# Routed expert blocks of a decoder layer: turning the token rows by VectorE instead of TensorE, and the order of the work beside it

## The reference, cut to what matters

```
x = x + mamba_branch(layernorm(x))                       # 8 x 512 tokens, 256 features
x = x + cross_attention(layernorm(x), ctx, ctx)
xf = layernorm(x)                                        # 4096 x 256
shared = gelu(xf @ Wfc_s + bfc_s) @ Wproj_s + bproj_s
topk_p, topk_i = top_k(softmax(xf @ Wr), 2)              # 2 of 8 experts, normalized
for e in range(8):
    h = gelu(xf @ Wfc[e] + bfc[e]) @ Wproj[e] + bproj[e] # 256 -> 1024 -> 256
    routed += h * gate[:, e]
x = x + shared + routed
```

## Time and profile before

| | |
|---|---|
| median of 3 runs | 934.13 us (933.46 to 935.68) |
| profiled execution | 939.65 us, span 938.0 us |
| TensorE busy, share of span | 901.5 us, 96% |
| VectorE busy | 611.6 us, 65% |
| ScalarE busy | 518.8 us, 55% |
| GpSimd busy | 338.4 us, 36% |
| mean granted clock | 0.99 |
| DMA | 64.0 MB in 48943 packets, mean 68 GB/s |

### The profile page before, as it was taken

How to read it: one execution, slowest core, us unless ns; L and a number is a source line. 1 busy time by engine, 2 the same in 40 slices (tenths; PEclk the granted TensorE clock), 3 DMA queues, 4 the chain that set the end, 5 groups by cost and what they waited for, 6 DMA issues and landing times.

```text
span 938.0 us, 20267 instructions
## 1 busy us (share of the span) xinstructions
PE 901.5 (96%) x6934; PEld 794.0 (85%) x6943; DVE 611.6 (65%) x1457; ACT 518.8 (55%) x1050; POOL 338.4 (36%) x318
## 2 busy tenths in 40 slices
PE   6999998999998999999999899999999999999996
PEld 4688995566655788888889899999999999999996
DVE  4898796898877766666555655565565656565442
ACT  3693433665546355546444666575666657575552
POOL 3467222211311554544453224233242423332222
PEclk9999999999999999999999899999999999999998
DMA  8300020000002111111237245225252522522222
GB/s 240 123 1 1 1 91 1 2 1 1 2 16 84 49 71 59 65 60 59 77 114 249 58 135 135 47 45 136 46 136 46 136 46 46 136 46 46 46 46 35
DMA packets 48943, 64.00 MB, mean 68 GB/s; under 512 B 9984, under 2 KB 41920, under 8 KB 48768
## 3 DMA queue, kind: packets, MB, share of 16 engines
q0 software_dynamic: 17504, 34.87, 16.0%
q1 hardware_dynamic: 31248, 27.46, 9.9%
q10 hardware_dynamic: 144, 1.05, 0.4%
HBM read 38.59 MB, written 24.77 MB: 68 GB/s over the span
## 4 chain that ended last, share of the span: by engine, by line
PE 86%; DVE 7%; issue 3%; ACT 1%; DMA 1%; POOL 1%; SPq 1%; DVEq 0%; POOLq 0%; ACTq 0%
PE PS L136 24%; PE PS L137 23%; PE PS L138 23%; PE PS L877 3%; PE PS L1833 2%; PE PS L306 2%; PE PS L907 1%; PE PS L921 1%; PE PS L927 1%; DVE mxpad L1121 1%; DVE hidl L142 1%; PE PS L287 1%; DMA xr<-routed_rows 1%; PE PS L1360 1%; PE PS L849 1%
## 5 line engine op out<-in xcount | busy, mean ns | idle before, releaser
L1879 ACT ACTIVATE hideh<-PS,be 128x256 fp32r<-128x256 f32 x280 | 140.5, 502 | 154.2 <-PE PS L138 139.5
L1907 POOL DMA_INDIRECT out_rows<-y,toki x70 | 122.9, 1755 | 270.4 <-DVE y L1947 261.3
L142 DVE TENSOR_TENSOR hidel<-act32e,hideh 128x256 fp32r<-128x256 f32 x280 | 118.4, 425 | 107.5 <-ACT act32e L1881 95.3
L136 PE MATMUL PS<-xTeh,wfch 128*128 128x256 f32 x560 | 159.4, 285 | 1.7 <-issue 1.1
L136 PE MATMUL PS<-wprh,hideh 128*128 128x256 f32 x560 | 159.0, 284 | 0.0
L137 PE MATMUL PS<-xTel,wfch 128*128 128x256 f32 x560 | 158.4, 283 | 0.0
L138 PE MATMUL PS<-xTeh,wfcl 128*128 128x256 f32 x560 | 158.4, 283 | 0.0
L138 PE MATMUL PS<-wprh,hidel 128*128 128x256 f32 x560 | 155.9, 278 | 0.0
L137 PE MATMUL PS<-wprl,hideh 128*128 128x256 f32 x560 | 155.9, 278 | 0.0
L1881 ACT ACTIVATE act32e<-PS,be 128x256 f32<-128x256 f32 x280 | 140.9, 503 | 2.8 <-DVE hidel L142 2.8
L136 PEld LDWEIGHTS PS<-xTeh,wfch 128*128 128x128 f32 x560 | 107.3, 192 | 3.3 <-issue 2.6
(11 more groups left out here) (273 smaller groups left out, 2086.3 us busy)
## 6 DMA issues: line engine op xcount, KB each, us to landing
xr<-routed_rows SPq DMA_DIRECT2D x36, 272.0 KB
fcraw<-in_Wfc POOLq DMA_DIRECT2D x8, 1024.0 KB
prraw<-in_Wproj POOLq DMA_DIRECT2D x8, 1024.0 KB
X<-in_x SPq DMA_DIRECT2D x8, 512.0 KB, 6.6
out_rows<-X SPq DMA_DIRECT2D x8, 512.0 KB, 2.9
routed_rows<-pads SPq DMA_DIRECT2D x8, 272.0 KB
out_rows<-y,toki POOLq DMA_INDIRECT x70
ctx<-in_ctxT SPq DMA_DIRECT2D x4, 256.0 KB, 6.5
```

Of the source, the lines that this page charges most:

```text
L136: nc.tensor.matmul(out, wh, xh, start=first, stop=False)
L142: return eng.tensor_tensor(out, whole, high.bitcast(F32), ALU.subtract)
L1879: nc.scalar.activation(hid[0][:, j, :], PS[:, j % 4, 0:BLK], ACT.Gelu_apprx_tanh, bias=bias)
L1907: nc.gpsimd.indirect_dma_start(out=out, out_offset=bass.IndirectOffsetOnAxis(ap=toki[:, h:h + 1], axis=0), in_=y[:, h, :], in_offset=None, ...
```

## The change

The rows of a block are loaded as four DMAs instead of one. DMA q takes features 64q to 64q+63 of all 256 rows and puts them on the partitions 32q to 32q+31, each partition holding eight pieces of 256 bytes. One VectorE transpose then turns every 32x32 square of the 128x512 tile in place on its partitions: partition 32q+f holds features of quarter q, for all 256 tokens. So the features come in another order than before, and the rows of `Wfc` are reordered to match on the host. x_high and take now read `xt` in SBUF. The gates and token numbers come by a small DMA of their own (64 bytes a row), which ACT issues at the head of each block. The gate copy and the two bias products move from behind the h_lows into the gaps between them; `toki` is copied after take, and only that copy waits for `y_sent`. The split is cut finer: ACT does one piece before x_high and three behind it, VectorE's `wprl` becomes two pieces, and its pieces stand between turn, take and the outputs.

```diff
+            xb = first_rows("xb", [P, BLK // SQ, KD * SQ])
+            metar = first_rows("metar", [P, 2, ROW - D])
+            rgx = RG.rearrange("(n t j) c -> n j t c", t=BLK // SQ, j=SQ)
...
-                sp.dma_start(xr[:], rg[0].rearrange("p h c -> p h c")).then_inc(x_in, 16)
+                for q in range(P // SQ):
+                    sp.dma_start(xb[q * SQ:(q + 1) * SQ],
+                                 rgx[0, :, :, q * KD * SQ:(q + 1) * KD * SQ]).then_inc(x_in, 16)
...
-                    if b == B - 1:
-                        routed_first()
...
                     def load(g, e, par, i):
                         sp.wait_ge(xr_free, g + 1)
-                        sp.dma_start(xr[:].rearrange("p (a h) c -> p a h c", a=1),
-                                     rg[bass.ds(e * NBR + i, 1)]...).then_inc(x_in, 16)
+                        for q in range(P // SQ):
+                            sp.dma_start(xb[q * SQ:(q + 1) * SQ]..., rgx[row, :, :, ...]...).then_inc(x_in, 16)
...
-                def transposes(pe, g):
-                    pe.wait_ge(x_in, g * 16 + 16)
-                    for k in range(KD):
-                        for h in range(2):
-                            last = nc.tensor.transpose(PS[:, 4, ...], xr[:, h, k * P:(k + 1) * P], ident[:])
+                def turn(dve, g):
+                    dve.wait_ge(x_in, g * X_IN + X_IN)
+                    nc.vector.transpose(xt[:]..., xb[:]...).then_inc(xr_free, 1)
...
                     def x_high(g):
-                        act.wait_ge(x_psum, g + 1)
-                        nc.scalar.activation(xTp[0][:]..., PS[:, 4, :], ACT.Copy).then_inc(xT_high, 1)
+                        act.wait_ge(xr_free, g + 2)
+                        nc.scalar.activation(squares(0), xt[:]..., ACT.Copy).then_inc(xT_high, 1)
...
                     def gelus(g, e, par, i):
+                        act.wait_ge(gate_ready, g + 1)
+                        nc.scalar.dma_start(metar[:]..., rg[bass.ds(e * NBR + i, 1), :, :, D:ROW]...).then_inc(meta_in, 16)
...
+                        with act.If(i * E + e < E - 1):
+                            act.wait_ge(raw_in, e * 32 + 64)
+                            split_up(1 - par, 0)
                         x_high(g + 1)
                         with act.If(i * E + e < E - 1):
-                            act.wait_ge(raw_in, e * 32 + 64)
-                            split_high(1 - par)
+                            split_up(1 - par, 1)
+                            split_down(1 - par)
...
+                        h_low(range(5))
+                        dve.wait_ge(meta_in, g * 16 + 16)
+                        nc.vector.tensor_copy(gate[:], metar[:, :, bass.ds(e, 1)]...).then_inc(gate_read, 1)
+                        h_low(range(5, 6))
+                        scale_bias(0)
+                        h_low(range(6, 7))
+                        scale_bias(1).then_inc(bias_gated, 1)
+                        h_low(range(7, KH))
+                        turn(dve, g + 1)
                         with dve.If(i * E + e < E - 1):
+                            up_low(0)
+                        take(dve, g + 1)
+                        dve.wait_ge(y_sent, g + 1)
+                        nc.vector.tensor_copy(toki[:], metar[:, :, E]).then_inc(gate_ready, 1)
...
```

More of the change, by code:

```diff
@@ L47, in build @@
     BLK = 2 * P
+    SQ = 32
     SQ = 32
@@ L1503, in whole @@
                         act.wait_ge(raw_in, 32)
-                        split_high(0)
+                        for k in range(KD):
+                            split_up(0, k)
+                        split_down(0)
                     if b < B - 1:
@@ L1823, in routed_sync, with squares, first_turn @@
                     load(before + count, E - 1, 1, 0)
-                    sp.wait_ge(x_in, (before + count) * 16 + 16)
+                    sp.wait_ge(x_in, (before + count) * X_IN + X_IN)
                     sp.sem_inc(sp_waits, 1)
-                def transposes(pe, g):
-                    pe.wait_ge(x_in, g * 16 + 16)
-                    if not isinstance(g, int):
-                        pe.wait_ge(xT_ready, g)
-                    for k in range(KD):
-                        for h in range(2):
-                            last = nc.tensor.transpose(PS[:, 4, k * BLK + h * P:k * BLK + (h + 1) * P],
-                                                       xr[:, h, k * P:(k + 1) * P], ident[:])
-                    last.then_inc(x_psum, 1)
+                xt = Place(rows_at)("xt", [P, BLK // SQ, KD, SQ])
+                def squares(n):
+                    return xTp[n][:].rearrange("p k (t j) -> p k t j", j=SQ)
+                def first_turn(dve):
+                    dve.sem_inc(xr_free, 1)
+                    turn(dve, 0)
+                def turn(dve, g):
+                    dve.wait_ge(x_in, g * X_IN + X_IN)
+                    nc.vector.transpose(xt[:].rearrange("p t k j -> p (t k j)"),
+                                        xb[:].rearrange("p t c -> p (t c)")).then_inc(xr_free, 1)
                 def take(dve, g):
-                    dve.wait_ge(x_psum, g + 1)
                     dve.wait_ge(xT_high, g + 1)
-                    low(nc.vector, xTp[1][:].rearrange("p k n -> p (k n)"), PS[:, 4, :],
-                        xTp[0][:].rearrange("p k n -> p (k n)")).then_inc(xT_ready, 1)
-                    nc.vector.tensor_copy(meta[:], xr[:, :, D:ROW]).then_inc(xr_free, 1)
+                    low(nc.vector, squares(1), xt[:].rearrange("p t k j -> p k t j"),
+                        squares(0)).then_inc(xT_ready, 1)
                 def routed_tensor(pe):
@@ new lines, in down_low @@
+                        def down_low(k):
+                            dve.wait_ge(e_high, e * 2 * KD + 3 * KD + k + 1)
+                            ks = slice(k * KH // KD, (k + 1) * KH // KD)
+                            return low(nc.vector, wpr[1][:, 1 - par, ks], prraw[:, ks], wpr[0][:, 1 - par, ks])
+                        h_low(range(5))
+                        dve.wait_ge(meta_in, g * 16 + 16)
+                        nc.vector.tensor_copy(gate[:], metar[:, :, bass.ds(e, 1)].rearrange("p h a -> p (h a)")).then_inc(
+                            gate_read, 1)
@@ new lines, in one @@
+                        dve.wait_ge(y_sent, g + 1)
+                        nc.vector.tensor_copy(toki[:], metar[:, :, E]).then_inc(gate_ready, 1)
+                        with dve.If(i * E + e < E - 1):
+                            up_low(1).then_inc(e_low, 1)
+                        dve.wait_ge(bias_gated, g + 1)
+                        output(0)
+                        with dve.If(i * E + e < E - 1):
+                            down_low(0)
+                        output(1)
+                        with dve.If(i * E + e < E - 1):
+                            down_low(1).then_inc(e_low, 1)
@@ L1954, in routed_vector @@
                     dve.sem_inc(l_ready, 2)
                     every_block(dve, one)
-                return (routed_sync, routed_tensor, routed_scalar, routed_gpsimd, routed_vector), transposes, take
-            routed, first_transposes, first_take = routed_stage()
+                return (routed_sync, routed_tensor, routed_scalar, routed_gpsimd, routed_vector), first_turn, take
+            routed, first_turn, first_take = routed_stage()
             with nc.Block() as block:
```

78 lines of the change are left out of this document (39 added, 39 removed).

## The result

| | before | after |
|---|---|---|
| median of the runs | 933.8 us (932.8 to 935.68, 4 runs) | 925.83 us (925.64 to 926.33, 4 runs) |
| profiled execution, its span | 939.65, 938.0 us | 925.91, 924.3 us |
| regular block, up + transposes + down | 5.76 + 0.35 + 5.55 = 11.66 us | 5.70 + 0 + 5.65 = 11.35 us |
| block 1 starts at | 529.59 | 522.74 |

The ratio is 0.99 (0.9881 to 0.992), a saving of 8.0 us. Forecast were 916.5, a saving of 17.6, and the range of 912 to 924 doesn't hold the time. The sign was right, the size not.

A forecast was written before the change was run, and what follows sets the result against it. The prediction took TensorE to bound the routed stage, waiting for nobody. It summed 15.0 us for 34 blocks and 2.6 for block 0 to 17.6, giving 934.13 - 17.6 = 916.5 us, with an 8-in-10 range of 912 to 924.

The forecast's parts named there:

- 34 x 0.44 = 15.0: Routed blocks 1 to 34: taking the transposes off TensorE saves 0.44 us in each, 15.0 us in all.
- Free: Small DMA on ACT, head of each block: its 0.39 us issue fits ScalarE's idle time before the first gelu.
- The term for block 0, 2.6: Block 0 and what leads up to it: block 1 starts 5.1 us earlier, about 2.5 comes back, 2.6 kept.
- Transposes on the path: Routed stage: each block's transposes stand in TensorE's chain as a piece of 0.44 us.
- Rival 1: Between up and down: a new wait takes the transposes' place; 931.5 us if all 0.44 returns, 924 if half; chance 0.08.
- Gate copy and bias products at nothing: Among the h_lows: gate copy and two bias products fit VectorE's 0.31 us gaps; cost nothing if nothing overlaps.
- Rival 3: Blocks behind a split or load, about 14: late ACT chain or late gates, some 1 us each; 930.5 us; chance 0.07.
- Turn, x_high, take: Between up and the next up: VectorE's turn, x_high and take stay hidden, at least 1.1 us to spare.
- Split at nothing: Weight split, cut finer: costs nothing; if the cover fails, at most 2.4 us in 7 blocks.
- rival 2: Row loads can't keep the pace: slower from landing times of 9.1 us or so, about 967 at 10; chance 0.06.
- the rule on 512 bytes: Row loads in 256-byte pieces: by the skill's rule they land later, block 0 gains only 0.2, total 918.9 us.
- The saving is taken over to the median: Final sum: the 17.6 us saving, counted on a profile 5.5 us above the median, is subtracted from median 934.13.

The follow-up runs named there:

- e2: Changed kernel with 128 unused bytes behind xb, putting the routed stage's tiles back at their old addresses; 926.38 us, ratio 0.9906.
- e3: Changed kernel with the gate copy and both bias products moved from among the h_lows to behind take; 924.19 us, ratio 0.9884.
- e7: Changed kernel with the small DMA issued by SP one block ahead and token numbers copied aside; 921.26 us, ratio 0.9853.
- e4: Changed kernel with four transposes of a constant tile put back on TensorE between up and down; 937.27 us, ratio 1.0027.
- e17: Changed kernel with 64 bytes ahead of the small tile and nothing else; 922.64 us, ratio 0.9862.
- e6: Changed kernel with VectorE's turn and its loads, but gate work, toki and the whole split behind the h_lows; 932.43 us, ratio 0.9972.
- e11: Changed kernel with gate copy and bias products still in the gaps, but the split in one piece as before; 932.49 us, ratio 0.9971.
- e12: Changed kernel with the split still spread, but gate copy, toki and bias products behind take; 923.53 us, ratio 0.9886.
- e10: Kernel before with its four transposes done twice in blocks 1 to 34; 946.8 us (one run).
- e9: Kernel before with the transposes of blocks 1 to 34 reading a constant tile instead of the rows; 932.46 us (one run).
- e13: Changed kernel with four constant transposes between up and down and 128 bytes ahead of the small tile; 932.79 us (one run).
- e14: Changed kernel with the small DMA on SP a block ahead, plus 64 bytes ahead of the small tile; 913.62 us (one run).
- e15: Changed kernel with the small DMA on SP a block ahead and 64 bytes ahead of the small tile, timed again in rounds; 916.11 us, ratio 0.9795.
- e5: Kernel before with the four transposes left out of every routed block, nothing else changed; 928.31 us, ratio 0.9912.
- e16: Changed kernel with the small DMA on SP a block ahead, xTe shifted by 64 bytes and hide by 128; 913.59 us, ratio 0.9778.
- e1: Kernel before, unchanged, run once more for a second profile; 934.65 us, span 933.0.

## Why the prediction failed

Two steps failed, of nearly equal size. Either alone would have left the time inside 912 to 924 (about 922); together they put it outside.

The first failed step is the term "34 x 0.44 = 15.0". It priced what leaves and took the spacing of what stays from the old stream ("Without transposes the distance is two steps", and "48 x 0.1135" for down without them). Measured: down's spacing goes from 0.1137 to 0.1177 when the transposes go (0.25 saved, not 0.44, by the removal alone), and up's from 0.120 to 0.1187 since the removed `metae` tile moves everything behind it by 128 bytes (e2 takes that back). That is 0.315 a block, 34 x 0.315 = 10.7, 4.3 less than the term.

The second failed step is the price of nothing for the gate work in the gaps ("if nothing overlaps: nothing") and for the small DMA ("Free"). It left out the wait for that DMA. Measured: five downs behind weight loads lose 3.85 us in the changed kernel's profile, and the losses go when the copy stands behind the h_lows (e3) or the DMA is issued a block earlier (e7).

The term for block 0, 2.6, came out near its size (2.85 won in block 0 against the second profile of before), but not by the path that was forecast; see below.

Point by point:

- **Transposes on the path:** right. They stood in TensorE's stream at 0.44 (doubled: +0.44).
- **Rival 1** (a wait takes their place): no wait came; the regular block has none. But a part of its price fell due by another mechanism: 0.13 of 0.44 came back in every block, as slower matmuls (0.19 in down, less 0.06 won in up). It asked only for waits, and the time came back as busy time.
- **Gate copy and bias products at nothing:** right for the copies themselves, wrong for the wait ahead of them. Rival 3 named it ("the gates land late under a weight load") but priced it in passing at 14 blocks of 1 us. It struck 5 downs, 3.85 us; in other profiles with the same small DMA the loss was 0.6 (e4) to 9.0 us (e17), so its size isn't a fixed one. With a chance of 0.07 and in none of the terms, it was missing from the sum. What I overlooked is that the wait for a DMA moved from behind the h_lows in among them, and that the DMA itself was new and late, issued in the block that needs it.
- **Turn, x_high, take:** right. VectorE's turn takes 0.70 at 727.58, take starts at 728.98, and TensorE's next up doesn't wait:

```profile
727.58 0.70 DVE L1851 STREAM_TRANSPOSE xt<-xb 128x512 f32<-128x512 f32 x1
728.98 0.69 DVE L143 TENSOR_TENSOR xTel<-xt,xTeh 128x512 fp32r<-128x512 f32 x1 [0.70 <-ACT xTeh L1886]
```

- **Split at nothing:** right as it was made, and the forecast didn't see how much hung on it: with the split in one piece the kernel is 6.6 to 8.9 us slower (e6, e11, e12). The pieces of 2.4 us in a row that stand ahead of the next h_lows in e6 show why.
- **The load** (rival 2, and the rule on 512 bytes): the turn waited for `xb` once, 0.2 us, between 515 and 920. Four times the pieces for the rows (87839 packets in all against 48943) made nothing else wait. By the Trainium skill (DMA: Bandwidth & Descriptors, Specifications) pieces under 512 bytes fall short of line rate; no row here shows a cost of it on the path for these loads. The gates' pieces of 64 bytes did come late, but beside a weight load, and no run separates the two.

```profile
DVE xt L1851 <- DMA xb<-routed_rows: 0.2, 1, 0.2
```

- **Block 0:** forecast start of block 1 at 524.5 with a pause of 1.9 and a half clock behind it; it started at 522.74, with no pause and no half clock. The rows were in at 519.59, not 521.8. What it is worth depends on which profile of before is set against it. Block 0 took 19.22 us in the earlier trace rows, 16.57 in the second profile and 13.72 after the change: 5.5 or 2.85. The gain is the pause of TensorE and the half clock behind it, which the changed kernel's profile hasn't; in an execution where they stay small there is less to gain (e10's block 0, at full clock, took 14.57 with its four transposes more). That 2.6 is near 2.85 is in part luck: the forecast took 5.1 from a profile slower than the median and gave 2.5 back for a half clock or waits in block 1; neither the pause nor the half clock came, and block 1 took 0.45 us over a regular one. **"The saving is taken over to the median"** was a third weak step: a profile 5.5 us above its median has a cause somewhere, and about half of it lay in just the stretch to which the forecast gave a gain.

```profile
519.59 0.71 DVE L1851 STREAM_TRANSPOSE xt<-xb 128x512 f32<-128x512 f32 x1 [0.18 <-DMA xb<-routed_rows]
```

The account, against the second profile of before: block 0 2.85, ahead of it -0.9 (a half clock that isn't the change's work), spacing and transposes 10.7, late gates -3.85; sum 8.8, measured 8.7 in the spans and 8.0 between the medians.

Not settled: why transposes ahead of down bring its spacing from 0.1177 to 0.1137 at one place of the tiles (e9, e10, e13) and not at the other (e4), why the same transposes take up from 0.1187 to 0.120 at that other place, and what it is in a place that counts. The steps within a product aren't equal but repeat: the changed kernel's up goes 115, 118, 121, 120, 119 ns over and over, and down of the kernel before starts with steps of 116 to 119 and then keeps 113 and 114. So the spacing depends on the place and on how the product was entered. The runs show the dependence only, in steps of 64 bytes and for `xTe` and `hide`; the weights and PSUM were never moved.

## What to carry to other kernels

When work leaves a saturated TensorE stream, measure the spacing of the matmuls that stay (first to first over the count), since busy time can take a gain back without a single wait in the list, and try the moving operand's tiles at other places, 64 bytes apart. A wait for a DMA that is moved ahead of work another engine needs must get an earlier issue with it: one block earlier, on SP, was worth 4.6 us here (3.85 of them the late gates). When a profile stands well above its median, find the stretch first; it may be the one you are about to claim.

## What the runs showed of the hardware

Mean spacing of a matmul of 256 columns with its 128x128 weight load, in regular blocks at granted clock 1.00, by the place of the moving operand's tiles against the changed kernel's. Behind transposes the first step, 0.20, is left out. Shift 0 is the changed kernel (behind transposes e4), 64 bytes e14, e15 and e17, 128 bytes e2 and e5, for down e16 too (behind transposes before, e9, e13):

| shift | up (xTe) | down (hide) | down behind transposes |
|---|---|---|---|
| 0 | 0.1187 us (0.120 with transposes between up and down) | 0.1177 us | 0.1177 us |
| 64 bytes | 0.1137 us | 0.120 us | not run |
| 128 bytes (as in before) | 0.120 us | 0.1177 us | 0.1137 us |

Between 0.1137 and 0.120 lie 5.5%, and over 34 blocks of 48 matmuls 34 x 48 x 0.0063 = 10 us for one product, more than the whole change saved. Two versions with the same instructions but 64 bytes of empty space differ by 5 us (e7 921.26 and e15 916.11; ratios 0.9853 and 0.9795).

Half clock, 3.4 or 6.8 us long, comes in some executions of a kernel and not in others at the same place: at 329 us in the first profile of before and after the change, but not in e1.
